# Recurrence stage: four row slots in place of three, the multipliers in the tile of the convolved rows

## The chip, the cores and the metric

The kernel is one launch on one core of one Trainium2 chip. The metric is the device time of the launch in microseconds, the median of several runs. Engines are named as the profile names them: PE (matmuls), DVE, ACT, POOL (vector, activation and general engines), SP (the queue that issues all DMAs here).

## The reference

Four sublayers, each followed by a residual add and a layer norm: a Mamba-2 mixer, a ternary linear layer with a bound on its norm, a gated linear recurrence, and a gated FFN with integer weight codes. The change is in the kernel's second stage, which computes sublayers two and three. Cut to what matters there:

```python
out = (x @ weight) * scale                       # then two factors per row from its norm
x = layernorm(x + bounded(out))                  # sublayer 2
y = gelu(x @ w_y + b_y);  xb = x @ w_x + b_x     # sublayer 3
conv = conv_b + sum(conv_w[k] * pad(xb)[:, k:k + Tn] for k in range(4))
gate_x = sigmoid(conv @ w_ig + b_ig);  gate_a = sigmoid(conv @ w_ag + b_ag)
log_a = -8 * gate_a * softplus(a_param);  a = exp(log_a)
mult = sqrt(1 - exp(2 * log_a))                  # 1 at the first row, where a = 0
h[t] = a[t] * h[t-1] + gate_x * conv * mult
x = layernorm(x + (h * y) @ w_out + b_out)
```

## The kernel before

`build` chains three stages that share the chip's memories: `mamba2`, `bounded_rg_lru` (the recurrence stage) and `gated_ffn`. Nothing is scheduled by a planner: each stage is five hand-written instruction streams, one per engine, joined by semaphores, and an engine runs its stream strictly in order. Stages overlap at their edges, because one stage's stream calls a few pieces of the following stage's.

The recurrence stage has NS = 8 steps, numbered 0 to 7; a step is 256 rows (two chunks of 128) of one of the two sequences, which alternate. Matmuls are split into high and low parts of the operands, three products for each. PE does in step s, in this order:

- `x` (L1502, `c_wx`): the projection w_x; `bounded(s+1)` (L1472, `c_wb`): the ternary layer of the next step; `y` (L1502, `c_wy`); `output(s-1)` (L1472, `c_wout`);
- `ag` (L1502, `c_wag`), which reads the convolved rows `c_cvh` and `c_cvl`; `turn(s+1)` (L1490), transposes; `ig` (L1502, `c_wig`); `turn_in(s+2)` (L1465), transposes of the raw rows of step s+2, one chunk after the other, as they were loaded into a row slot.

The elementwise chain that runs beside it: ACT makes the sigmoid `gx` (L1234) after `ig`, the exponentials `a` (L1243), the copy `c_bxh` of the transposed rows (L1211); POOL multiplies `gx` by the convolved rows `cv` (L1193, signal `s_gc`); DVE squares `a` into `mu` (`squared`, L1357); ACT takes the root in place (L1289, `s_mu`); at the top of the next step DVE (`recur`) multiplies `gx` by `mu` (L1363, `s_hchain`), scans (L1366) and multiplies by `y` (L1370); ACT and DVE split that into `c_hyh` (L1229) and `c_hyl` (L1374) for `output`; ACT rewrites `cv` for the new step (L1258), DVE adds three taps (`convolve`, L1342), ACT and DVE make `c_cvh` (L1273) and `c_cvl` (L1350) for `ag`.

In step 7 ACT makes `a` before `gx`. POOL's multiplication is then the last input that `recur(7)` waits for. Behind step 7, PE has the FFN's first three gate/up blocks `gate_up(0, 0..2)` (L1853), then `output(7)`. The gate part of block 2 waits for the FFN's first activation `d_sg` (ACT, L1753, behind the root of step 7), and its up part for the FFN's first product `d_h` (DVE, L1796, `product(0,0)`, behind `recur(7)`).

Row slots: a step's raw rows lie in a slot from their load to the step's normalised result. With three slots, the load of step s+3 is issued by SP when the result of step s (`s_ln`) is written, one step ahead of its `turn_in`. Results of steps whose slot is used again go through the tile `ob`.

Of the kernel before, what the change touches and what calls it, by code (L numbers as in the profile page):

```python
# [5 lines left out]
P = 128  # L6
D = 512
# [993 lines left out]
def bounded_rg_lru(nc, signals, psum, ident, powers, x_in, x_out, scale, vectors, b_out, W, split, last, spaces, room, ahead):  # L1001
# [5 lines left out]
    T = 256  # L1007
# [2 lines left out]
    NT = x_in.shape[0] // (B * C)  # L1010
    NS = B * NT
    M = KD
    SLOTS = 3
    TINY = 1e-7
    LIMIT = 0.99
    def sem(name):
# [37 lines left out]
    gx = sb_main("c_gx", [P, M, T], F32)  # L1054
    a = sb_main("c_a", [P, M, T], F32)
    room["mu"] = sb_main.at
    mu = sb_main("c_mu", [P, M, T], F32)
    xpre = sb_main("c_xpre", [P, M, T + 3], F32)
    xb.append(sb_main("c_xb2", [P, C, D], F32))
    bo = sb_main("c_bo", [P, D], F32)  # L1060
    room["end"] = sb_main.at
    hs = gx

    ps_t = psum[:, 0:2].rearrange("p j (k t) -> p j k t", k=KD)
    ps_o = psum[:, 2:4]
# [1 line left out]
    ps_b = psum[:, 6:8].rearrange("p q (m t) -> p q m t", m=2)  # L1067

    s_small, s_bias, s_const, s_sp, s_sp_act = (sem(n) for n in ("small", "bias", "const", "sp", "sp_act"))
    s_x = [[sem(f"x{i}_{j}") for j in range(C)] for i in range(SLOTS)]  # L1070
    s_st = [sem(f"st{j}") for j in range(C)]
    s_bt, s_bh, s_bl, s_bm, s_ob, s_ssq, s_nm, s_th, s_f = (sem(n) for n in ("bt", "bh", "bl", "bm", "ob", "ssq", "nm", "th", "f"))
    s_bvar, s_bstd, s_bln = sem("bvar"), sem("bstd"), sem("bln")
# [13 lines left out]
        return slice(j * P, (j + 1) * P)  # L1087

    def slot(s):
        return xb[s % SLOTS]  # L1090

    def finished(s):
        return ob if s + SLOTS < NS else slot(s)

    def sync(sp):
        def load_x(s):
            for j in range(C):
                wait(sp, s_ln, C * (s - SLOTS) + j + 1)
                sp.dma_start(slot(s)[:, j, :], chunk(x_in, s, j)).then_inc(s_x[s % SLOTS][j], 16)

        def store(s):
            for j in range(C):
                sp.wait_ge(s_ln, C * s + j + 1)
                sp.dma_start(chunk(x_out, s, j), finished(s)[:, j, :]).then_inc(s_st[j], 16)

        def constants():
            sp.dma_start(vec, vectors).then_inc(s_small, 16)
            sp.dma_start(scl, scale.partition_broadcast(P)).then_inc(s_small, 16)

        def main(following_stage):  # L1110
            sp.wait_ge(*last["output"])
            sp.dma_start(bo, b_out.partition_broadcast(P)).then_inc(s_bias, 16)
            load_x(2)
            for dst, src, arrived in ahead:
                sp.dma_start(dst, src).then_inc(arrived, 16)
            for s in range(NS - 2):
                if s + SLOTS < NS:
                    load_x(s + SLOTS)
                store(s)
            following_stage["small"]()  # L1120
            following_stage["load_x"](0)
            following_stage["gate_codes"]()
            store(NS - 2)
            following_stage["up_codes"]()
            following_stage["load_r"](0, 0)
            following_stage["load_r"](0, 1)
            store(NS - 1)
            following_stage["down_codes"]()
            for j in range(C):
                sp.wait_ge(s_st[j], 16 * NS)  # L1130

        return {"load_x": load_x, "constants": constants, "main": main}

    def gpsimd(pool):
        order = Order(pool, s_pool)

        def constants():
            pool.wait_ge(*last["gate"])
            pool.memset(hlast, 0.0).then_inc(s_const, 1)

        def bound(s):
            pool.wait_ge(s_ssq, C * s + C)
            order(pool.tensor_tensor(nrm, ssq, powers[:, 2:3].broadcast_to([P, C]), ALU.pow))
            pool.tensor_scalar(nm, nrm, TINY, None, ALU.max).then_inc(s_nm, 1)
            pool.wait_ge(s_nm, s + 1)
            order(pool.tensor_scalar(f, nm, TINY, None, ALU.add))
            order(pool.tensor_tensor(f, f, powers[:, 3:4].broadcast_to([P, C]), ALU.pow))
            pool.wait_ge(s_th, s + 1)
            order(pool.tensor_tensor(f, f, th, ALU.mult))
            order(pool.tensor_tensor(g, f, nrm, ALU.mult))  # L1150
            order(pool.tensor_scalar(g, g, TINY, None, ALU.max))
            order(pool.tensor_tensor(g, g, powers[:, 3:4].broadcast_to([P, C]), ALU.pow))
            order(pool.tensor_scalar(g, g, LIMIT, 1.0, ALU.mult, ALU.min))
            pool.tensor_tensor(f, f, g, ALU.mult).then_inc(s_f, 1)

        def bounded_norm(s):
            for j in range(C):
                pool.wait_ge(s_bvar, C * s + j + 1)
                inverse_root(pool, order, bmv[:, j, 1:2], powers, bmv[:, j, 2:3]).then_inc(s_bstd, 1)

        def norm(s):
            for j in range(C):
                pool.wait_ge(s_var, C * s + j + 1)
                inverse_root(pool, order, mv[:, j, 1:2], powers, mv[:, j, 2:3]).then_inc(s_std, 1)

        def out_bias(s):
            for j in range(C):
                pool.wait_ge(s_xt, C * s + j + 1)
                pool.tensor_tensor(slot(s)[:, j, :], slot(s)[:, j, :], bo, ALU.add).then_inc(s_bo, 1)

        def edges(s):
            wait(pool, s_conv, s)
            if s < B:
                pool.memset(xpre[:, :, 0:3], 0.0).then_inc(s_edge, 1)
            else:
                pool.tensor_copy(xpre[:, :, 0:3], carry[:, s % B]).then_inc(s_edge, 1)
            pool.wait_ge(s_edge, 2 * s + 1)
            pool.wait_ge(s_pre, M * s + M)
            pool.tensor_copy(carry[:, s % B], xpre[:, :, T:T + 3]).then_inc(s_edge, 1)

        def main(following_stage):
            pool.wait_ge(s_bias, 16)
            pool.wait_ge(*last["output"])
            out_bias(0)
            for s in range(NS):
                edges(s)
                if s + 1 < NS:
                    bound(s + 1)
                    bounded_norm(s + 1)
                if s:  # L1190
                    norm(s - 1)
                pool.wait_ge(s_gx, M * s + M)
                pool.tensor_tensor(gx, gx, cv, ALU.mult).then_inc(s_gc, 1)  # L1193
                if s < B:
                    wait(pool, s_hchain, s)
                    pool.memset(mu[:, :, 0:1], 1.0).then_inc(s_one, 1)
                if s + 1 < NS:
                    out_bias(s + 1)
            for m in range(EARLY):
                following_stage["low"](0, m)  # L1200
            norm(NS - 1)

        return {"constants": constants, "bound": bound, "bounded_norm": bounded_norm, "main": main}

    def scalar(act):
# [39 lines left out]
        def main(following_stage):  # L1245
            act.wait_ge(s_sp, 3)
            for s in range(NS):
                wait(act, s_conv, s)
                wait(act, s_edge, 2 * s)
                for m in range(M):  # L1250
                    act.wait_ge(s_xb, 2 * s + m // 2 + 1)
                    act.activation(xpre[:, m, 3:T + 3], ps_a[:, m // 2, m % 2, :], ACT.Identity,
                                   bias=vec[:, BX, m:m + 1]).then_inc(s_pre, 1)
                wait(act, s_gc, s)
                wait(act, s_cvl, s)
                act.wait_ge(s_pre, M * s + M)
                for m in range(M):
# [42 lines left out]
    def vector(dve):  # L1300
# [7 lines left out]
        def scaled(s):  # L1308
            if s == 0:
                dve.wait_ge(s_small, 32)  # L1310
            for j in range(C):
                dve.wait_ge(s_bm, C * s + j + 1)
                wait(dve, s_st[j], 16 * (s - SLOTS + 1))
                dve.tensor_tensor(ob[:, j, :], ps_o[:, j, :], scl, ALU.mult).then_inc(s_ob, 1)

        def bounded(s):
            dve.wait_ge(s_f, s + 1)
            for j in range(C):
                own = slot(s)[:, j, :]
                dve.wait_ge(s_x[s % SLOTS][j], 16 * (s // SLOTS + 1))  # L1320
                order(dve.scalar_tensor_tensor(out=own, in0=ob[:, j, :], scalar=f[:, j:j + 1], in1=own, op0=ALU.mult, op1=ALU.add))
                order(dve.bn_stats(bstats[:, j, :], own))
                dve.memset(hold, 0.0)
                dve.bn_aggr(bmv[:, j, 0:2], bstats[:, j, :]).then_inc(s_bvar, 1)
# [131 lines left out]
    def tensor(pe):  # L1456
        def turn_in(s):
            for j in range(C):
                pe.wait_ge(s_x[s % SLOTS][j], 16 * (s // SLOTS + 1))
                if s:  # L1460
                    pe.wait_ge(s_xl, C * (s - 1) + j + 1)
                else:
                    pe.wait_ge(*last["transposes"])
                for k in range(KD):
                    done = pe.transpose(ps_t[:, j, k, :], slot(s)[:, j, k * P:(k + 1) * P], ident)  # L1465
                done.then_inc(s_bt, 1)
# [559 lines left out]
```

## Time and profile before

| | |
|---|---|
| median of 3 runs | 1135.15 us (1133.3 to 1135.44) |
| the profiled execution, its own time | 1135.18 us |
| its span, first to last instruction | 1133.1 us |
| PE busy | 1071.9 us, 95% |
| DVE, ACT, POOL busy | 749.0 (66%), 574.2 (51%), 319.3 us (28%) |
| mean granted PE clock | 0.983 |
| the recurrence stage | about 462 to 769 us of the span |

Two microseconds of the device time lie outside the span. Shares of busy time are means over three stages; what a change in the recurrence stage is worth is read from the waits of that stage. Matmul ends are modelled, and consecutive matmuls overlap by their pipelining, so start times are what is compared.

### The profile page before, as it was taken

What the parts mean: (1) busy time and instruction counts of PE and PEld (TensorE: products, weight loads), DVE (VectorE), ACT (ScalarE), POOL (GpSimd) and SP (SyncE); (2) the same over time, 40 slices, a digit from 0 to 9 for tenths busy, and PEclk for the clock granted to TensorE, in tenths of its full rate; (3) what the DMA queues carried; (4) which work ended last, traced back from release to release, by engine and by line L of the source; (5) the groups of instructions that cost most, each with busy time, mean ns of one, the idle gap of its engine ahead of it and who ended that gap; (6) DMA issues with size and microseconds to landing.
All of it is one profiled execution on the core that took longest, in us unless ns stands there. A gap on an engine that the chain in (4) does not pass through costs nothing.

```text
span 1133.1 us, 18155 instructions
## 1 busy us (share of the span) xinstructions
PE 1071.9 (95%) x6912; PEld 934.0 (82%) x6912; DVE 749.0 (66%) x1311; ACT 574.2 (51%) x1190; POOL 319.3 (28%) x433
## 2 busy tenths in 40 slices
PE   6889999999999997889999999899999999999997
PEld 6778888888888885788998998887888888888886
DVE  6899999999999998657766687765432133223213
ACT  6856767676767673645665556563212311321220
POOL 1012223130313214343434444313312321321331
PEclk9899999999999999989999999999999999999999
DMA  5504031322313056501011101408012002002001
GB/s 197 199 3 147 31 116 47 101 60 87 108 39 127 2 201 196 194 2 29 11 38 38 38 1 38 140 19 282 15 38 75 1 19 93 1 1 75 1 1 56
DMA packets 41590, 81.22 MB, mean 72 GB/s; under 512 B 7456, under 2 KB 13472, under 8 KB 39456
## 3 DMA queue, kind: packets, MB, share of 16 engines
q1 hardware_dynamic: 41504, 80.06, 21.2%
q8 instruction: 55, 0.90, 0.3%
q14 instruction: 31, 0.25, 0.1%
HBM read 67.19 MB, written 12.85 MB: 71 GB/s over the span
## 4 chain that ended last, share of the span: by engine, by line
PE 60%; DVE 24%; ACT 7%; issue 5%; POOL 2%; DMA 1%; DVEq 0%; SPq 0%; POOLq 0%; ACTq 0%
PE banks L1853 20%; PE banks L801 12%; PE banks L1866 10%; PE banks L1502 8%; DVE a_L L658 4%; DVE a_xs L575 3%; PE banks L1472 3%; PE banks L931 2%; DVE c_gx L1366 1%; DVE c_cv L1342 1%; PE banks L923 1%; DVE a_L L672 1%; ACT c_a L1243 1%; DVE a_ygl L701 1%; PE banks L881 1%
## 5 line engine op out<-in xcount | busy, mean ns | idle before, releaser
L1753 ACT ACTIVATE d_sg<-banks,d_gs 128x512 f32<-128x512 f32 x64 | 44.0, 688 | 224.8 <-PE banks L1853 224.8
L1796 DVE SCALAR_TENSOR_TENSOR d_h<-banks,d_us,d_sg 128x512 f32<-128x512 f32 x64 | 48.1, 751 | 163.6 <-PE banks L1853 151.3
L1727 POOL TENSOR_TENSOR d_hl<-d_h,d_hh 128x512 fp32r<-128x512 f32 x64 | 83.2, 1300 | 158.3 <-ACT d_hh L1757 158.2
L575 DVE SCALAR_TENSOR_TENSOR a_xs<-a_xpre,a_cvec,a_xs 128x256 f32<-128x256 f32 x192 | 100.3, 537 | 6.4 <-ACT a_xs L446 1.8
L1866 PE MATMUL banks<-d_wd,d_hh 128*128 128x512 f32 x256 | 101.1, 395 | 0.0
L1866 PE MATMUL banks<-d_wd,d_hl 128*128 128x512 f32 x256 | 100.9, 394 | 0.0
L331 POOL TENSOR_TENSOR a_sg<-a_sg 128x512 f32<-128x512 f32 x16 | 24.5, 1533 | 221.8 <-ACT a_sg L438 221.8
L658 DVE TENSOR_TENSOR_SCAN a_L<-a_L,a_ident 128x512 f32<-128x512 f32 x64 | 78.4, 1225 | 2.2
L801 PE MATMUL banks<-a_xth,a_wxh 128*128 128x256 f32 x256 | 75.7, 296 | 0.4 <-DVE a_wxl L566 0.4
L462 ACT ACTIVATE a_xdt<-banks,a_dt 128x64 f32<-128x64 f32 x256 | 56.5, 349 | 36.4 <-PE banks L881 36.4
L801 PE MATMUL banks<-a_xth,a_wgh 128*128 128x256 f32 x256 | 74.9, 293 | 0.0
L801 PE MATMUL banks<-a_xtl,a_wxh 128*128 128x256 f32 x256 | 73.4, 287 | 0.0
L801 PE MATMUL banks<-a_xth,a_wxl 128*128 128x256 f32 x256 | 73.3, 286 | 0.0
L801 PE MATMUL banks<-a_xth,a_wgl 128*128 128x256 f32 x256 | 72.7, 284 | 0.0
L801 PE MATMUL banks<-a_xtl,a_wgh 128*128 128x256 f32 x256 | 72.7, 284 | 0.0
L801 PE MATMUL banks<-a_woh,a_ygh 128*128 128x512 f32 x128 | 54.2, 423 | 5.4 <-ACT a_gs L426 3.5
L1866 PEld LDWEIGHTS banks<-d_wd,d_hl 128*128 128x128 f32 x256 | 48.1, 188 | 11.2
L1866 PEld LDWEIGHTS banks<-d_wd,d_hh 128*128 128x128 f32 x256 | 48.2, 188 | 11.0
L801 PEld LDWEIGHTS banks<-a_xth,a_wxh 128*128 128x128 f32 x256 | 49.6, 194 | 5.1 <-issue 4.1
L801 PE MATMUL banks<-a_woh,a_ygl 128*128 128x512 f32 x128 | 52.1, 407 | 0.0
L801 PE MATMUL banks<-a_wol,a_ygh 128*128 128x512 f32 x128 | 52.0, 406 | 0.0
L1853 PE MATMUL banks<-d_xtl,d_wg_late 128*128 128x512 f32 x128 | 51.5, 402 | 0.0
(285 smaller groups left out, 3144.6 us busy)
## 6 DMA issues: line engine op xcount, KB each, us to landing
a_L<-decays SPq DMA_DIRECT2D x16, 1024.0 KB, 5.1
a_xf<-in_x SPq DMA_DIRECT2D x16, 256.0 KB, 2.9
a_xr<-in_x SPq DMA_DIRECT2D x16, 256.0 KB, 2.7
tokens<-a_xr SPq DMA_DIRECT2D x16, 256.0 KB, 4.0
c_xb<-tokens SPq DMA_DIRECT2D x16, 256.0 KB, 3.2
d_xin<-tokens SPq DMA_DIRECT2D x16, 256.0 KB, 5.0
d_r<-tokens SPq DMA_DIRECT2D x16, 256.0 KB, 2.7
d_wd_codes<-in_down_w SPq DMA_DIRECT2D x4, 1024.0 KB, 9.1
```

The costliest lines, as they stand in the source:

```text
L331: order(pool.tensor_tensor(sq[:, 0:4], sq[:, 0:4], sq[:, 4:8], ALU.add))
L462: ins = act.activation(xdt[:, j, h * HD:(h + 1) * HD], ps_t[:, q % 2, 2 * j + i // 2, i % 2 * HD:(i % 2 + 1) * HD], ACT.Copy, scale=dt[:, ...
L575: ins = dve.scalar_tensor_tensor(out=dst, in0=src[:, k:k + T], scalar=vec[:, k:k + 1], in1=dst, op0=ALU.mult, op1=ALU.add)
L658: order(dve.tensor_tensor_scan(own, own, ident4.rearrange("p h t -> p (h t)"), 0.0, ALU.mult, ALU.add))
L801: last = pe.matmul(out, lhs(i, k), rhs(c, k), start=(k, i, c) == (0, 0, 0), stop=(k, i) == (n - 1, 1))
L1472: done = pe.matmul(ps_x, x[:, k, cols(j)], wp[:, k, :], start=i == 0, stop=i == 3 * KD - 1)
L1502: done = pe.matmul(ps_x[:, q, m % 2, :], wp[:, k, m * P:(m + 1) * P], x[:, k, :], start=i == 0, stop=i == 3 * KD - 1)
L1727: pool.tensor_tensor(hl[:, m, :], h32[:, m % 2, :], hh[:, m, :].bitcast(F32), ALU.subtract).then_inc(s_hl, 1)
L1753: act.activation(sg[:, m % 2, :], ps_g[:, m % 2, :], ACT.Silu, scale=gs[:, m:m + 1]).then_inc(s_sg, 1)
L1796: dve.scalar_tensor_tensor(out=h32[:, m % 2, :], in0=ps_u[:, m % 2, :], scalar=us[:, m:m + 1], in1=sg[:, m % 2, :], op0=ALU.mult, op1=ALU. ...
L1853: ins = pe.matmul(out[:, m % 2, :], w(k, m), x[:, k, :], start=(k == 0 and x is xth), stop=(k == KD - 1 and x is xtl))
L1866: ins = pe.matmul(ps_o[:, c % 2, :], h[:, m, cols(c)], wd[:, m, :], start=(m == 0 and h is hh), stop=(m == M - 1 and h is hl))
```

## The change

A fourth row slot `c_xb3` takes the place of the tile `mu`, and `mu` becomes another name of the tile `cv`. The table `SLOT` says which slot a step uses. From this follow the waits: `squared(s)` and the memset of the first column overwrite `cv`, so they wait until POOL's multiplication has read it (`s_gc`); ACT's rewrite of `cv` in the next step waits until `recur` has read the multipliers (`s_hchain`).

```diff
-    SLOTS = 3
+    SLOT = (0, 1, 2, 3, 0, 2, 1, 0)
...
-    mu = sb_main("c_mu", [P, M, T], F32)
+    xb3 = sb_main("c_xb3", [P, C, D], F32)
     xpre = sb_main("c_xpre", [P, M, T + 3], F32)
-    xb.append(sb_main("c_xb2", [P, C, D], F32))
+    xb += [sb_main("c_xb2", [P, C, D], F32), xb3]
...
     hs = gx
+    mu = cv
...
+    def use(s):
+        return SLOT[:s + 1].count(SLOT[s])
+
+    following_use = {s: SLOT.index(SLOT[s], s + 1) for s in range(NS) if SLOT[s] in SLOT[s + 1:]}
+    earlier_use = {n: s for s, n in following_use.items()}
 
     def finished(s):
-        return ob if s + SLOTS < NS else slot(s)
+        return ob if s in following_use else slot(s)
...
             load_x(2)
+            load_x(3)
...
             for s in range(NS - 2):
-                if s + SLOTS < NS:
-                    load_x(s + SLOTS)
+                if s in following_use:
+                    load_x(following_use[s])
                 store(s)
...
             following_stage["up_codes"]()
+            store(NS - 1)
+            following_stage["down_codes"]()
+            for j in range(C):
+                sp.wait_ge(s_st[j], 16 * NS)
             following_stage["load_r"](0, 0)
             following_stage["load_r"](0, 1)
-            store(NS - 1)
-            following_stage["down_codes"]()
-            for j in range(C):
-                sp.wait_ge(s_st[j], 16 * NS)
...
                 if s < B:
-                    wait(pool, s_hchain, s)
+                    pool.wait_ge(s_gc, s + 1)
                     pool.memset(mu[:, :, 0:1], 1.0).then_inc(s_one, 1)
...
                 wait(act, s_gc, s)
+                wait(act, s_hchain, s)
                 wait(act, s_cvl, s)
...
         def squared(s):
             dve.wait_ge(s_a, M * s + M)
+            dve.wait_ge(s_gc, s + 1)
```

On SP the row loads move. In these rows `c_xb_132` is slot 0, `c_xb_138` slot 1, `c_xb_165` slot 2, `c_xb_163` the new slot 3; `tokens` is the array of rows in the chip's main memory. Before, from the load of step 2 to the store of step 5:

```order
L1099 DMA c_xb_165<-tokens 128x512 x2
...
L1099 DMA c_xb_132<-tokens 128x512 [waits c_ln] x2
L1104 DMA tokens<-c_ob 128x512 [waits c_ln] x2
L1099 DMA c_xb_138<-tokens 128x512 [waits c_ln] x2
L1104 DMA tokens<-c_ob 128x512 [waits c_ln] x2
L1099 DMA c_xb_165<-tokens 128x512 [waits c_ln] x2
L1104 DMA tokens<-c_ob 128x512 [waits c_ln] x2
L1099 DMA c_xb_132<-tokens 128x512 [waits c_ln] x2
L1104 DMA tokens<-c_ob 128x512 [waits c_ln] x2
L1099 DMA c_xb_138<-tokens 128x512 [waits c_ln] x2
L1104 DMA tokens<-c_ob 128x512 [waits c_ln] x2
```

The same place after the change, to the store of step 4:

```order
L1107 DMA c_xb_165<-tokens 128x512 x2
L1107 DMA c_xb_163<-tokens 128x512 x2
...
L1107 DMA c_xb_132<-tokens 128x512 [waits c_ln] x2
L1112 DMA tokens<-c_ob 128x512 [waits c_ln] x2
L1107 DMA c_xb_138<-tokens 128x512 [waits c_ln] x2
L1112 DMA tokens<-c_ob 128x512 [waits c_ln] x2
L1107 DMA c_xb_165<-tokens 128x512 [waits c_ln] x2
L1112 DMA tokens<-c_ob 128x512 [waits c_ln] x2
L1112 DMA tokens<-c_xb_163 128x512 [waits c_ln] x2
L1107 DMA c_xb_132<-tokens 128x512 [waits c_ln] x2
L1112 DMA tokens<-c_ob 128x512 [waits c_ln] x2
```

The loads before are those of steps 2, 3, 4, 5, 6, 7. After, step 3's goes out with step 2's; the next is step 4's (behind the result of step 0), then step 6's (behind that of step 1), step 5's (behind step 2) and step 7's (behind step 4). So steps 3, 4 and 6 are loaded earlier than before, 5 and 7 behind the same result as before.

On DVE no instruction moves; a wait is added. Here is the end of step 7 with the recurrence behind it, before:

```order
L1790 TENSOR_TENSOR d_xtl<-banks,d_xth 128x4x128 [waits d_xh] x2
L1357 TENSOR_TENSOR c_mu<-c_a 128x1024 [waits c_a]
L1363 TENSOR_TENSOR c_gx<-c_gx,c_mu 128x1024 [waits c_gc,c_mu]
L1366 SCALAR_TENSOR_TENSOR c_gx<-c_a,c_hlast,c_gx 128x256 [waits c_hchain]
L1366 SCALAR_TENSOR_TENSOR c_gx<-c_a,c_hlast,c_gx 128x256 x3
L1368 COPY c_hlast<-c_gx 128x4 [waits c_dve_order]
L1370 TENSOR_TENSOR c_gx<-c_gx,c_y 128x1024 [waits c_y,c_dve_order]
L1796 SCALAR_TENSOR_TENSOR d_h_181<-banks,d_us,d_sg 128x512 [waits d_u,d_sg]
```

The same rows after:

```order
L1801 TENSOR_TENSOR d_xtl<-banks,d_xth 128x4x128 [waits d_xh] x2
L1368 TENSOR_TENSOR c_cv<-c_a 128x1024 [waits c_gc,c_a]
L1374 TENSOR_TENSOR c_gx<-c_gx,c_cv 128x1024 [waits c_gc,c_mu]
L1377 SCALAR_TENSOR_TENSOR c_gx<-c_a,c_hlast,c_gx 128x256 [waits c_hchain]
L1377 SCALAR_TENSOR_TENSOR c_gx<-c_a,c_hlast,c_gx 128x256 x3
L1379 COPY c_hlast<-c_gx 128x4 [waits c_dve_order]
L1381 TENSOR_TENSOR c_gx<-c_gx,c_y 128x1024 [waits c_y,c_dve_order]
L1807 SCALAR_TENSOR_TENSOR d_h_181<-banks,d_us,d_sg 128x512 [waits d_u,d_sg]
```

The square now stands behind POOL's product (`c_gc`) as well as behind `a`, and writes `c_cv`.

## Rows read from the trace of the kernel before

**Rows 1.** Timeline, PE: turn_in matmuls behind a load; start, length in us, [idle before]
```profile
538.50 0.66 PE L1465 MATMUL banks<-ident,c_xb 128*128 128x128 f32 x4 [1.34 <-DMA c_xb<-tokens]
...
611.19 0.65 PE L1465 MATMUL banks<-ident,c_xb 128*128 128x128 f32 x4 [0.95 <-DMA c_xb<-tokens]
...
647.19 0.66 PE L1465 MATMUL banks<-ident,c_xb 128*128 128x128 f32 x4 [0.42 <-DMA c_xb<-tokens]
```

**Rows 2.** Timelines of ACT and PE: where ag begins in steps 2, 3, 5
```profile
558.78 1.06 ACT L1273 ACTIVATE c_cvh<-c_cv 128x1024 fp32r<-128x1024 f32 x1 [1.29 <-DVE c_cv L1342]
561.29 0.64 PE L1502 MATMUL banks<-c_cvh,c_wagh 128*128 128x256 f32 x4
567.05 1.03 PE L1490 MATMUL banks<-ident,c_xb 128*128 128x128 f32 x8
...
595.82 1.06 ACT L1273 ACTIVATE c_cvh<-c_cv 128x1024 fp32r<-128x1024 f32 x1 [1.28 <-DVE c_cv L1342]
596.93 0.74 PE L1502 MATMUL banks<-c_cvh,c_wagh 128*128 128x256 f32 x4
603.08 1.04 PE L1490 MATMUL banks<-ident,c_xb 128*128 128x128 f32 x8
...
668.39 1.06 ACT L1273 ACTIVATE c_cvh<-c_cv 128x1024 fp32r<-128x1024 f32 x1 [1.28 <-DVE c_cv L1342]
669.89 0.64 PE L1502 MATMUL banks<-c_cvh,c_wagh 128*128 128x256 f32 x4
```

**Rows 3.** Timelines of POOL and DVE: product by cv and the square, steps 3, 6
```profile
610.76 2.38 POOL L1193 TENSOR_TENSOR c_gx<-c_gx,c_cv 128x1024 f32<-128x1024 f32 x1 [3.37 <-ACT c_gx L1234]
615.43 1.29 DVE L1357 TENSOR_TENSOR c_mu<-c_a 128x1024 f32<-128x1024 f32 x1
...
720.56 2.40 POOL L1193 TENSOR_TENSOR c_gx<-c_gx,c_cv 128x1024 f32<-128x1024 f32 x1 [3.36 <-ACT c_gx L1234]
723.54 1.75 DVE L1357 TENSOR_TENSOR c_mu<-c_a 128x1024 f32<-128x1024 f32 x1 [4.56 <-ACT c_a L1243]
```

**Rows 4.** Timelines of ACT and DVE: cv rewritten, top of step 7
```profile
727.96 2.08 ACT L1258 ACTIVATE c_cv<-c_xpre,c_vec 128x256 f32<-128x256 f32 x4
728.73 1.21 DVE L1363 TENSOR_TENSOR c_gx<-c_gx,c_mu 128x1024 f32<-128x1024 f32 x1
734.15 1.06 ACT L1229 ACTIVATE c_hyh<-c_gx 128x1024 fp32r<-128x1024 f32 x1 [4.12 <-DVE c_gx L1370]
```

**Rows 5.** Timelines of DVE, POOL, ACT and PE: behind step 7
```profile
755.49 1.23 DVE L1357 TENSOR_TENSOR c_mu<-c_a 128x1024 f32<-128x1024 f32 x1 [4.50 <-ACT c_a L1243]
758.42 2.42 POOL L1193 TENSOR_TENSOR c_gx<-c_gx,c_cv 128x1024 f32<-128x1024 f32 x1 [9.21 <-ACT c_gx L1234]
759.65 1.06 ACT L1289 ACTIVATE c_mu<-c_mu 128x1024 f32<-128x1024 f32 x1
760.94 1.23 DVE L1363 TENSOR_TENSOR c_gx<-c_gx,c_mu 128x1024 f32<-128x1024 f32 x1 [4.23 <-POOL c_gx L1193]
766.26 0.74 DVE L1796 SCALAR_TENSOR_TENSOR d_h<-banks,d_us,d_sg 128x512 f32<-128x512 f32 x1
767.06 0.50 PE L1853 MATMUL banks<-d_xth,d_wu_early 128*128 128x512 f32 x1 [0.49 <-DVE d_h L1796]
```

**Rows 6.** Windows: us, busy of PE, PEld, DVE, ACT, POOL, PE clock, DMA
```profile
479.34:487.00 7.66, 5.65 (x45) 5.45 (x46) 5.75 (x4) 4.00 (x7) 6.10 (x6) 1.00 0.31 120
737.00:740.00 3.00, 3.00 (x9) 2.33 (x9) 2.93 (x8) 2.07 (x5) 0.00 (x0) 0.59 0.00 0
775.00:1120.00 345.00, 345.00 (x1507) 279.01 (x1507) 105.65 (x184) 80.34 (x134) 90.09 (x91) 1.00 0.13 45
```

**Rows 7.** Timeline, PE: first matmul of output(6), in step 7
```profile
736.52 0.79 PE L1472 MATMUL banks<-c_wouth,c_hyh 128*128 128x512 f32 x1 [4.70 <-DVE c_hyl L1374]
```

**Rows 8.** Timeline, SP: last store; the tile view, DVE: first use of d_r
```profile
776.89 1.58 SPq L1104 DMA_DIRECT2D tokens<-c_xb  x2
...
L1804 DVE TENSOR_TENSOR d_r<-d_r,d_tmp x16: 691/692/693, 834.6 to 1127.5; 128x512 f32<-128x512 f32 x16
```

More of the change, by code:

```diff
@@ L1069, in bounded_rg_lru @@
     s_small, s_bias, s_const, s_sp, s_sp_act = (sem(n) for n in ("small", "bias", "const", "sp", "sp_act"))
-    s_x = [[sem(f"x{i}_{j}") for j in range(C)] for i in range(SLOTS)]
+    s_x = [[sem(f"x{i}_{j}") for j in range(C)] for i in range(len(xb))]
     s_st = [sem(f"st{j}") for j in range(C)]
@@ L1089, in slot @@
     def slot(s):
-        return xb[s % SLOTS]
+        return xb[SLOT[s]]
+    def use(s):
+        return SLOT[:s + 1].count(SLOT[s])
+    following_use = {s: SLOT.index(SLOT[s], s + 1) for s in range(NS) if SLOT[s] in SLOT[s + 1:]}
+    earlier_use = {n: s for s, n in following_use.items()}
     def finished(s):
-        return ob if s + SLOTS < NS else slot(s)
+        return ob if s in following_use else slot(s)
     def sync(sp):
@@ L1097, in load_x @@
             for j in range(C):
-                wait(sp, s_ln, C * (s - SLOTS) + j + 1)
-                sp.dma_start(slot(s)[:, j, :], chunk(x_in, s, j)).then_inc(s_x[s % SLOTS][j], 16)
+                if s in earlier_use:
+                    sp.wait_ge(s_ln, C * earlier_use[s] + j + 1)
+                sp.dma_start(slot(s)[:, j, :], chunk(x_in, s, j)).then_inc(s_x[SLOT[s]][j], 16)
         def store(s):
@@ L1124, in main @@
             following_stage["up_codes"]()
-            following_stage["load_r"](0, 0)
-            following_stage["load_r"](0, 1)
             store(NS - 1)
@@ L1130, in main @@
                 sp.wait_ge(s_st[j], 16 * NS)
+            following_stage["load_r"](0, 0)
+            following_stage["load_r"](0, 1)
         return {"load_x": load_x, "constants": constants, "main": main}
@@ L1312, in scaled @@
                 dve.wait_ge(s_bm, C * s + j + 1)
-                wait(dve, s_st[j], 16 * (s - SLOTS + 1))
+                wait(dve, s_st[j], 16 * (s - 2))
                 dve.tensor_tensor(ob[:, j, :], ps_o[:, j, :], scl, ALU.mult).then_inc(s_ob, 1)
@@ L1319, in bounded @@
                 own = slot(s)[:, j, :]
-                dve.wait_ge(s_x[s % SLOTS][j], 16 * (s // SLOTS + 1))
+                dve.wait_ge(s_x[SLOT[s]][j], 16 * use(s))
                 order(dve.scalar_tensor_tensor(out=own, in0=ob[:, j, :], scalar=f[:, j:j + 1], in1=own, op0=ALU.mult, op1=ALU.add))
@@ L1458, in turn_in @@
             for j in range(C):
-                pe.wait_ge(s_x[s % SLOTS][j], 16 * (s // SLOTS + 1))
+                pe.wait_ge(s_x[SLOT[s]][j], 16 * use(s))
                 if s:
```

## The prediction

> **What bounds the kernel now.** I began with the granted clock and PE's busy share, then asked for the stretch behind the recurrence: from 775 to 1120 us PE is busy 345.00 of 345.00 us at clock 1.00 [rows 6]. So whatever moves the start of that stretch moves the end of the kernel by as much, and the question is only what PE loses before it.
>
> The waits for row loads came next. In the timeline of PE the second chunk of `turn_in` sits behind the load in four places: 1.34 us for step 3's rows, 0.95 for step 5's, 0.42 for step 6's [rows 1], and one like these for step 7's. Step 4's rows come in time. That is what a fourth slot can attack.
>
> Last, what would stop PE if a load did not. `ag` needs `c_cvh` from the chain through DVE and ACT. In step 2 `c_cvh` is ready at 558.78 + 1.06 = 559.84, and `ag` starts at 561.29, because PE itself is late, by the wait of 1.34. In step 3 it is ready at 596.88 and `ag` starts at 596.93: here the chain sets the pace, with the load of step 4's rows in time [rows 2]. There is a second cost in that state. `c_cvl` comes one DVE instruction after `c_cvh`, so `ag`, which runs 567.05 - 561.29 = 5.76 us when both are ready, takes 603.08 - 596.93 = 6.15 us [rows 2]. PE and the chain are level within a few tenths, so neither alone is the bound.
>
> **The change part by part.**
>
> *Loads of steps 3, 4 and 6 earlier.* Step 3's wait of 1.34 us goes. `ag` of step 2 could start at 561.29 - 1.34 = 559.95; the chain allows 559.84 [rows 1, 2]. The chain does not gain from the early load: it starts from `ig`, and the raw rows enter it only with `c_bxh`, which ACT copies behind the exponentials anyway. So `ag` gains 1.34, and is now as close behind `c_cvh` as in step 3, which costs it most of 6.15 - 5.76 = 0.39; I take 0.34. Net 1.0 us. Step 4's early load removes no wait. For step 6, 0.42 us goes: `ag` of step 5 starts at 669.89 with `c_cvh` ready at 669.45, so it can move 0.42, and then pays the same stall of nearly 0.39 [rows 1, 2]. Net 0.05. The waits for steps 5 and 7 stay: their loads go out behind the same results, and these move with PE. Sum: **-1.0 us**. Bounds: -1.76 if every removed microsecond counts (1.34 + 0.42), -0.6 if a second stall of 0.39 shows up.
>
> The Trainium skill has a rule for this, in "DMA: Bandwidth & Descriptors", Rules for kernel authors: issue a DMA early and wait late, so that its fixed cost overlaps. Its "Perfetto Trace Analysis", Optimization Strategy, adds that the same gap repeated on the saturated engine can mean too few buffers. Both read these gaps as a buffer shortage; by them the gain would be the whole 1.76 us, where the rows on `c_cvh` leave 1.0.
>
> *The square behind POOL's product, steps 0 to 6.* In steps 0 to 5 DVE first makes the low part of step s+2's rows. In step 3 POOL ends at 610.76 + 2.38 = 613.14 and the square starts at 615.43, a margin of 2.3 us. In step 6 there is no such work; POOL ends at 722.96, the square starts at 723.54, a margin of 0.58 [rows 3]. Cost nothing; without that cover step 6 would pay what POOL is late, in the chain to `output(6)`. In steps 0 and 1 DVE already waits for the memset behind the same product.
>
> *The rewrite of `cv` behind `s_hchain`.* In ordinary steps DVE's product by `mu` runs while ACT makes four `xpre`, so nothing is late. At the top of steps 6 and 7 DVE converts FFN weights first. For step 7 the product ends at 728.73 + 1.21 = 729.94, so ACT starts `cv` then and not at 727.96 and ends near 732.0. ACT's next work, `c_hyh`, starts at 734.15 after 4.12 us of idleness [rows 4]. Hidden; `convolve` comes later still.
>
> *The square behind POOL's product, step 7.* Here `gx` is made last, so the order inverts. Before: square at 755.49, root at 759.65, both finished (760.71) when POOL's product ends at 758.42 + 2.42 = 760.84; DVE's product starts at 760.94 [rows 5]. After: the square starts behind 760.84, takes 1.23; the root takes 1.06; with the handovers of a few hundredths each the product starts at about 763.3. That is 2.35 us later. `recur(7)` has no slack: `d_h` at 766.26 follows it, and PE waits for it already, 0.49 us, at 767.06 [rows 5]. So the up part of block 2 starts near 769.4. The activations behind the root are late by about as much, which delays the gate part of the same block less than that; it adds nothing to the sum. `c_hyl` is ready before that up part ends, as now. Sum: **+2.35 us**. Bounds: +2.29 (1.23 + 1.06, no handover) to +2.8, if half a microsecond is lost at the following products.
>
> *SP.* One load more stands ahead of the FFN's early codes, which DVE converts only in steps 5 and 6. The FFN's first residual rows `d_r` move behind the last store. That store is issued at 776.89, and the first use of `d_r` is at 834.6 [rows 8]: even several microseconds for the down codes and the landing leave some 45. Late up codes wait for `s_hy` of step 7, 2.35 - 1.0 us later, and PE, which wants them later by the same amount, never waits in that stretch [rows 6]. Cost nothing.
>
> **Sum:** 1135.18 (the profiled execution's own time: span 1133.1 and 2.1 around it) - 1.0 + 2.35 = **1136.5 us**. The median of the runs shown, 1135.15, is the same within 0.03, so this is also the forecast of the median: 0.12% slower, within the 0.2% (2.3 us) that a measurement of this kernel can tell from no change.
>
> **The rivals.**
>
> *The clock falls in the new gap (slower).* The place is block 2 of the FFN behind step 7: PE's 0.49 us of idleness grows to about 2.8, in two pieces around the gate part. After 4.70 us of idleness ahead of `output(6)` [rows 7] the granted clock from 737 to 740 is 0.59, which means mostly the lower level, 1.2 GHz [rows 6]; with the half microsecond ahead of it that costs about 3.0 x 0.41 + 0.25 = 1.5 us. Against it: with 7.66 - 5.65 = 2.0 us idle in one stretch the clock stayed at 1.00 [rows 6]. The new gap lies between. If it falls: 1136.5 + 1.5 = 1138.0 us, 0.25% slower. It decides as soon as the fall costs over 0.9 us. The Trainium skill, "TensorE: Matmul & The Clock Gate", HAM oscillation, warns of this: gaps put the array back to half rate and each return is paid again. It speaks against the change; the row on `output(6)` agrees. Chance 0.2.
>
> *All the removed waits count.* If `ag` does not pay for `c_cvl`, or the chain moves with PE, the gain is 1.76: 1135.8 us. For it: the wait of 1.34 disappears in full. Against it: `ag` in step 3. Chance 0.13.
>
> *The end of step 7 is hidden (faster or level).* If PE's work behind step 7 absorbs the late root, the sum is 1134.2 us, and with all waits counted 1133.4. For it: two and a half gate/up blocks stand between `ig` and the first instruction that needs it. Against it: PE waits for `d_h` already now. Chance 0.1.
>
> *The added waits show in other steps.* A late POOL product in step 6, or DVE and POOL in each other's way, since a square of 1.29 us takes 1.75 there [rows 3]. Half a microsecond in two or more steps: 1137.5 to 1138.5 us. Chance 0.1.
>
> *The change doesn't do what it says:* the rows of steps 3 and 6 still arrive late. They are issued a step or more earlier, so this would need a stuck queue; then 1137.5. Chance 0.02.
>
> **How the numbers follow.** The forecast has 0.45. Runs before spread over 2.1 us, and half-rate stretches of PE fall differently in each run, so each case carries about 1 us to either side. The range 1134.2 to 1138.7 reaches from the hidden end to the fallen clock with a little over. Slower by over 0.2% (above 1137.4): most of the clock's 0.2, half of the added waits and a sixth of the forecast, 0.29. Faster by over 0.2% (below 1132.9): a part of the hidden end, 0.06. The rest, 0.65, is within.
>
> **What would show it.** In the profile after: no idle PE at `turn_in` for steps 3 and 6, some 1 us for 5 and 7; `ag` of steps 2 and 5 starting within 0.1 us of `c_cvh` and taking about 6.1 us; the start of `ig` in step 3 one microsecond earlier. In step 7, the square starting as POOL's product ends, and PE idle over 2 us ahead of the up part of block 2. The prediction is wrong if that gap is not there, if PE's clock drops behind it, or if the square waits for POOL in steps 1 to 6.

## The result, and the profile after

In the comparison of the two kernels, twelve runs of each, the changed one took 1137.87 us (median; 1136.12 to 1139.52) and the one before 1134.31 us (1132.73 to 1135.44). The ratio is 1.0026, 95% interval 1.0017 to 1.0036: slower by about 0.26%. (The medians alone lie 3.56 us apart, 0.31%. Each ratio in this text comes with its interval from the record and is not the quotient of the medians beside it.) The profiled execution took 1136.12 us, with a span of 1134.4 us.

First the loads. Timeline of PE after the change, all waits for row loads that are left from `turn_in(3)` to the end of step 6 (start, length in us; idle time before in brackets), and the first matmuls of `turn_in(6)`:

```profile
610.05 0.66 PE L1476 MATMUL banks<-ident,c_xb 128*128 128x128 f32 x4 [1.01 <-DMA c_xb<-tokens]
...
645.03 1.04 PE L1476 MATMUL banks<-ident,c_xb 128*128 128x128 f32 x8
...
682.62 0.66 PE L1476 MATMUL banks<-ident,c_xb 128*128 128x128 f32 x4 [0.96 <-DMA c_xb<-tokens]
```

Steps 3 and 6 no longer wait, steps 5 and 7 still do [rows 1]. Timelines of ACT and PE, where `ag` begins in step 2 and in step 5:

```profile
558.58 1.06 ACT L1283 ACTIVATE c_cvh<-c_cv 128x1024 fp32r<-128x1024 f32 x1 [1.29 <-DVE c_cv L1352]
559.70 0.74 PE L1513 MATMUL banks<-c_cvh,c_wagh 128*128 128x256 f32 x4
...
667.23 1.06 ACT L1283 ACTIVATE c_cvh<-c_cv 128x1024 fp32r<-128x1024 f32 x1 [1.28 <-DVE c_cv L1352]
668.35 0.75 PE L1513 MATMUL banks<-c_cvh,c_wagh 128*128 128x256 f32 x4
```

In step 2 `c_cvh` is ready at 559.64 and `ag` starts 0.06 us later, where 1.45 us lay between before [rows 2]; the stage's next section (`turn`) starts at 565.85, so `ag` takes 6.15 us and not 5.76.

Now the end of step 7. Timelines of POOL, DVE, ACT and PE:

```profile
757.24 2.42 POOL L1202 TENSOR_TENSOR c_gx<-c_gx,c_cv 128x1024 f32<-128x1024 f32 x1 [9.19 <-ACT c_gx L1243]
...
759.76 1.23 DVE L1368 TENSOR_TENSOR c_cv<-c_a 128x1024 f32<-128x1024 f32 x1 [9.94 <-POOL c_gx L1202]
762.12 1.22 DVE L1374 TENSOR_TENSOR c_gx<-c_gx,c_cv 128x1024 f32<-128x1024 f32 x1 [1.13 <-ACT c_cv L1299]
767.43 0.74 DVE L1807 SCALAR_TENSOR_TENSOR d_h<-banks,d_us,d_sg 128x512 f32<-128x512 f32 x1
...
761.02 1.06 ACT L1299 ACTIVATE c_cv<-c_cv 128x1024 f32<-128x1024 f32 x1 [2.57 <-DVE c_cv L1368]
...
764.23 0.47 PE L1864 MATMUL banks<-d_xth,d_wg_early 128*128 128x512 f32 x1 [0.70 <-ACT d_sg L1764]
768.23 0.50 PE L1864 MATMUL banks<-d_xth,d_wu_early 128*128 128x512 f32 x1 [1.90 <-DVE d_h L1807]
```

The square stands behind POOL's product and the root behind the square. From the end of POOL's product (759.66) to DVE's product by the multipliers it is 2.46 us, where it was 0.10 [rows 5]. PE idles 0.70 us ahead of the gate part of block 2 and 1.90 us ahead of its up part, where it was 0.49 in all. By start times, which don't hang on modelled ends, `output(7)` follows `gate_up(0,0)` by 14.29 us (770.19 - 755.90) and not by 11.96 (769.03 - 757.07).

Windows behind the gap (busy PE, PEld, DVE, ACT, POOL; granted clock; DMA). In this execution the clock stays up:

```profile
768.00:773.00 5.00, 4.77 (x21) 3.88 (x22) 2.82 (x4) 2.97 (x5) 3.47 (x3) 1.00 0.85 274
773.00:777.00 4.00, 4.00 (x19) 3.22 (x18) 2.54 (x6) 0.00 (x0) 1.68 (x3) 1.00 0.49 185
```

The median of the changed kernel lies 1.75 us above this execution. Two parts of the program are therefore measured apart in every profile below, and both are free of what happens ahead of the stage. **A** runs from the first matmul of `turn_in(3)` to the first matmul of `gate_up(0,0)` (the end of `ig` in step 7), **B** from there to the end of the span. (Spans are printed to a tenth, so differences of up to 0.1 us in B are rounding.) Here A went from 220.51 to 219.74 and B from 376.03 to 378.50.

| kernel | span | A | B | `output(7)` takes | clock fell behind the gap |
|---|---|---|---|---|---|
| before | 1133.1 | 220.51 | 376.03 | 5.56 | no |
| changed | 1134.4 | 219.74 | 378.50 | 5.60 | no |
| changed, again (`after_again`) | 1138.2 | 219.53 | 380.10 | 6.71 | yes |
| changed, third | 1135.9 | 219.85 | 380.01 | 6.53 | yes |
| changed, fourth | 1137.5 | 219.82 | 380.08 | 6.06 | yes |
| `mu_only` | 1134.4 | 220.41 | 378.54 | 5.60 | no |
| `early5` | 1136.7 | 219.20 | 380.00 | 6.62 | yes |
| `filled`, three profiles | 1135.9, 1135.1, 1132.4 | 219.79, 219.96, 219.89 | 378.39, 378.49, 378.43 | 5.56, 5.60, 5.60 | no |
| `last_mu` | 1130.9 | 219.78 | 376.03 | 5.55 | no |
| `last_mu_convert` | 1126.5 | 217.47 | 376.12 | 5.56 | no |
| `all_three` | 1131.2 | 217.00 | 376.12 | 5.56 | no |
| `before_convert` | 1128.6 | 218.09 | 376.11 | 5.55 | no |

What is left of each span, its start to `turn_in(3)`, is 532.9 to 538.6 us in these 14 executions, although the code there is all but the same. It is why a single time says little here, and A and B much. Steps 0 and 1, where the memset of the first column has a new wait too, lie in that part. From the first matmul of `x(0)` to `turn_in(3)` the twelve profiles with the shared tile took 72.0 to 75.1 us and the two without it 74.3 and 74.6, at mean clocks of 0.93 to 0.98: no cost of the change is seen there, and one of some tenths could not be.

### The profile page after: what moved, and what is told of

Its sections match the earlier page's. It is cut to its first block, busy times and chain, and to the rows that moved or that the text cites. A ratio compares the mean times of both kernels' runs of the same rounds, so it can differ in the third digit from the quotient of the medians.

```text
span 1134.4 us, 18168 instructions
## 1 busy us (share of the span) xinstructions
PE 1078.2 (95%) x6912; PEld 939.1 (83%) x6912; DVE 749.5 (66%) x1311; ACT 573.3 (51%) x1190; POOL 320.5 (28%) x433
## 4 chain that ended last, share of the span: by engine, by line
PE 59%; DVE 25%; ACT 6%; issue 6%; POOL 2%; DMA 1%; DVEq 0%; SPq 0%; POOLq 0%; ACTq 0%
PE banks L1864 20%; PE banks L1877 10%; PE banks L1513 10%; PE banks L801 9%; DVE a_L L658 5%; PE banks L1483 5%; DVE a_xs L575 4%; PE banks L931 2%; DVE a_ygl L701 1%; DVE a_L L672 1%; DVE c_gx L1377 1%; PE banks L923 1%; DVE c_cv L1352 1%; ACT c_a L1252 1%; DVE a_ex L646 1%
## 5 line engine op out<-in xcount | busy, mean ns | idle before, releaser
L1864 PE MATMUL banks<-d_xth,d_wu_early 128*128 128x512 f32 x128 | 50.7, 396 | 1.9 <-DVE d_h L1807 1.9
```

The costliest lines, as they stand in the source:

```text
L1864: ins = pe.matmul(out[:, m % 2, :], w(k, m), x[:, k, :], start=(k == 0 and x is xth), stop=(k == KD - 1 and x is xtl))
```

## The experiments

The theory was that of the prediction: the early loads are worth under a microsecond, the serial end of step 7 costs 2.35, and the rest is the clock or noise. The rivals: all waits count; the added waits cost in other steps too; the clock falls in the new gap.

**The changed kernel again** (`after_again`; no edit).

> The changed kernel once more, for a second profile and more times. In its first profile the recurrence gains 0.8 us and the end of step 7 loses 2.35 us, which is +1.2 to +1.5 us on the time before, but the medians of twelve runs lie 3.5 us apart. Theory A (the clock falls behind the new gap in part of the executions): +2 to +4 us in the median, and the profile shows either a clock of 1.00 in the first blocks of the FFN and a time near the low end, or one near half for some microseconds and a time about 1.5 us higher. Theory B (the two medians lie apart because of the stage before, whose half-rate stretches differ by run): the median comes back to +1 to +2 us, with no difference behind step 7 between the profiles.

It took 1136.7 us against 1134.77, ratio 1.0012 (0.9998 to 1.0026). Its profile has the same gaps, 0.70 and 1.90 us, but behind them:

```profile
770.00:775.00 5.00, 4.57 (x14) 3.64 (x15) 3.01 (x4) 3.16 (x5) 3.26 (x3) 0.69 0.83 262
775.00:779.00 4.00, 4.00 (x18) 3.27 (x17) 1.56 (x4) 0.00 (x0) 1.39 (x3) 0.96 0.52 201
```

A clock of 0.69 means that much of the window ran at 1.2 GHz: 14 matmuls in place of 21. `output(7)` takes 6.71 us, B is 1.6 us longer than in the first profile. The rival's fall does happen, in some executions. The difference of the medians, 1.93 us, lies just below what the first theory asked for and within what the second did; the profile decides, since behind step 7 the two executions differ.

**Only the shared tile** (`mu_only`): three slots in the order of before, `mu` in `cv`. Like all edits but that of `before_convert`, this one is made to the changed kernel.

```diff
-    SLOT = (0, 1, 2, 3, 0, 2, 1, 0)
+    SLOT = (0, 1, 2, 0, 1, 2, 0, 1)
...
-            load_x(3)
```

> The multipliers share the tile of the convolved rows, but rows are loaded into three slots in the order of the kernel before. By the prediction's sum: +2.35 us on the kernel before, and up to 1.5 us more if the clock falls behind the gap; PE's waits for loads as before (1.3, 0.0, 0.9, 0.4, 1.0 us). If the loss belonged to the loads, this kernel would be within 0.5 us of the kernel before.

1136.5 us, ratio 1.0023 (1.0009 to 1.0037). A is 220.41, within 0.1 of before: the waits that the shared tile adds in steps 2 to 6 cost nothing. PE waits 1.16, 0.21, 1.02, 0.48 and 1.12 us for the rows of steps 3 to 7, near the 1.3, 0.0, 0.9, 0.4 and 1.0 expected. B is 378.54, the whole 2.5 us. So A's gain in the changed kernel belongs to the slots, and B's loss to the shared tile.

**Step 7's multipliers in another tile** (`last_mu`): in step 7 alone they lie in slot 3, which is free by then, and the square does not wait.

```diff
-    mu = cv
+    multipliers = [cv] * (NS - 1) + [xb3.rearrange("p c (m t) -> p (c m) t", m=M // C)]
...
-            dve.wait_ge(s_gc, s + 1)
+            if multipliers[s] is cv:
+                dve.wait_ge(s_gc, s + 1)
```

> As the changed kernel, but step 7 squares into the fourth slot, which is free by then, and does not wait for POOL's product; steps 0 to 6 keep their multipliers in the tile of the convolved rows. By the prediction's sum the 2.35 us behind step 7 are gone and the gain of the early loads stays: 0.6 to 1.2 us faster than the kernel before, 2.3 us or, with a clock that falls behind the gap, up to 4 us faster than the changed one. PE waits about 0.5 us for the first FFN product, as before. The rival, that the loss comes from the early load of step 3 at the head of the stage or from the waits in steps 0 to 6, expects no or little gain on the changed kernel.

1132.88 us, ratio 0.9980 (0.9969 to 0.9991): faster than before. Timelines of DVE, ACT, POOL and PE at the end of its step 7:

```profile
753.29 1.23 DVE L1369 TENSOR_TENSOR c_xb<-c_a 128x1024 f32<-128x1024 f32 x1 [4.50 <-ACT c_a L1252]
758.74 1.23 DVE L1375 TENSOR_TENSOR c_gx<-c_gx,c_xb 128x1024 f32<-128x1024 f32 x1 [4.22 <-POOL c_gx L1202]
...
757.45 1.06 ACT L1299 ACTIVATE c_xb<-c_xb 128x1024 f32<-128x1024 f32 x1
...
756.21 2.42 POOL L1202 TENSOR_TENSOR c_gx<-c_gx,c_cv 128x1024 f32<-128x1024 f32 x1 [9.21 <-ACT c_gx L1243]
...
764.86 0.50 PE L1865 MATMUL banks<-d_xth,d_wu_early 128*128 128x512 f32 x1 [0.49 <-DVE d_h L1808]
```

Square and root are done before POOL's product ends, as in the kernel before [rows 5], PE waits 0.49 us, and B is 376.03, as before, while A keeps the gain of the slots. One wait in one step is the whole loss. By A and B alone it should win 0.73 us over before. The timed 1.9 us is more than that and than the 0.6 to 1.2 expected, and the interval ends at 1.0; what the rest is stays open.

**Step 5's rows a step earlier** (`early5`): the slot order (0, 1, 2, 3, 0, 1, 2, 0), all else as changed.

> As the changed kernel with the slots in the order 0, 1, 2, 3, 0, 1, 2, 0, so that step 5's rows are loaded one step earlier as well; step 7's stay late. This takes away the wait of 1.0 us in step 3. If the chain through DVE and ACT sets the pace where PE does not wait (the prediction), ag of step 4 moves by 0.95 us, pays 0.3 to 0.4 of it for the low part, and the kernel gains 0.5 to 0.7 us on the changed one. If every removed wait counts in full, it gains 1.0 us.

1136.86 us, ratio 1.0013 (1.0002 to 1.0024). Of the four waits at `turn_in` only step 7's is left, 1.15 us. A is 219.20, between 0.33 and 0.65 us better than in the four profiles of the changed kernel; expected were 0.5 to 0.7. The time is no lower than that of the changed kernel. The clock fell again.

**Dummy matmuls in the gap** (`filled`): two ahead of the gate part of block 2, seven ahead of its up part; work that is added, and nothing reads what it writes.

```diff
+                    if i == 0 and m == 2:
+                        for _ in range(2 if out is ps_g else 7):
+                            pe.matmul(psum[:, 0], w(0, m), xth[:, 0, :], start=True, stop=True)
                     pe.wait_ge(used, M * i + m - 1)
```

> The changed kernel with nine matmuls more, whose results nothing reads: two ahead of the gate part and seven ahead of the up part of the FFN's block 2, inside the gaps of 0.7 and 1.9 us that PE has there. Same waits, about 1.9 us less idleness. In two of four profiles with the gap left open the clock fell behind it and cost 1.5 us. If the idleness is what makes it fall, this profile shows the clock at 1.00 from the first FFN block to the end of output(7), and the median is 0.4 to 1.0 us below that of the changed kernel. If the fall has another cause, half of such profiles fall still, and the median is the same or 0.1 us higher.

1136.33 us against 1134.21, ratio 1.0016 (1.0002 to 1.003). Expected was a median 0.4 to 1.0 us below that of the changed kernel. That did not come out: the medians lie 2.12 us above before with the gap filled and 1.93 or 3.56 with it open, and these differ by less than the intervals are wide, so the timed runs don't decide. Its profile:

```profile
763.00:768.00 5.00, 4.86 (x22) 3.59 (x21) 4.16 (x7) 3.25 (x4) 0.00 (x0) 1.00 0.00 0
768.00:773.00 5.00, 4.67 (x21) 3.47 (x20) 3.91 (x5) 2.79 (x4) 1.93 (x2) 1.00 0.54 142
773.00:777.00 4.00, 4.00 (x19) 3.27 (x18) 2.09 (x5) 0.63 (x1) 2.89 (x4) 1.00 0.89 342
```

PE is busy through the gap, the up part waits 0.33 us, and the clock is 1.00.

**How often it falls.** Two more profiles each of the changed kernel and of the filled one, one execution each:

> The changed kernel once more, one profile. The question is how often the granted clock falls behind the gap of some 2.6 us ahead of the up part of block 2. If the fall is a matter of chance from execution to execution, as two profiles of four so far say, either outcome can come: 1.00 in the windows behind the gap and about 366.1 us from the up part to the end of the span, or a window below 0.95 and about 367.7 us.

> The changed kernel with nine dummy matmuls in the gap, one profile. If idleness of PE is what lets the clock fall, the clock is 1.00 in every window of block 2 and output(7), and output(7) takes 5.6 us, as in its first profile. If the fall comes whatever PE does there, it is seen in about half of the profiles, and output(7) takes 6.2 to 6.7 us.

> As the third profile of the changed kernel: a fall costs about 1.5 us behind the up part of block 2, no fall costs nothing; with a chance near one half, one of the two further profiles should show it.

> As the second profile of the kernel with dummy matmuls: clock 1.00 and 5.6 us for output(7) if idleness is the cause; three profiles without a fall beside about half of the open ones with one would be weak evidence for it, one fall would refute it.

Windows of PE alone (busy, clock, DMA share, GB/s) behind the gap, of the changed kernel's third profile:

```profile
766.00:768.00 2.00, 0.33 (x2) 1.00 0.00 0
768.00:771.00 3.00, 2.77 (x9) 0.75 0.76 186
771.00:774.00 3.00, 3.00 (x10) 0.68 0.99 369
774.00:777.00 3.00, 3.00 (x15) 1.00 0.37 150
```

and of its fourth:

```profile
769.50:772.50 3.00, 2.75 (x8) 0.66 0.67 182
772.50:775.50 3.00, 3.00 (x12) 0.77 1.00 377
```

With the two further ones of the filled kernel at 1.00 throughout, the count is: gap open (changed kernel four times, `mu_only`, `early5`), four falls in six; gap filled, none in three; gap as before (before, `last_mu` and three below), none in five. The cost of a fall is B's step from 378.5 to between 380.0 and 380.1, 1.5 to 1.6 us, each time. Three filled profiles against six open ones are few: had the fall come with its rate of four in six whatever PE does, three without one would have a chance of 1 in 27; if only the four falls in these nine profiles are taken as given, the chance that all four land among the six open ones is 15 in 126, one in eight. With the five profiles of a short gap counted as well, four in six beside none in eight, it is 15 in 1001. So that the fall goes with the wider gap is well borne out, and that PE's idleness is what matters in that gap is likely, not shown.

**The conversions ahead of the square.** In steps 5 and 6 DVE converts FFN weights between the square and the product. Here it does so before `turn_in` and the square, where it idles 4.56 us for `a` [rows 3], together with `last_mu` (`last_mu_convert`), with that and the slots of `early5` (`all_three`), and alone in the kernel before (`before_convert`).

```diff
+                if NS - 4 < s < NS - 1:
+                    for i in range(4 * (s - NS + 3), 4 * (s - NS + 4)):
+                        following_stage["convert"](i)
                 if s + 2 < NS:
                     turn_in(s + 2)
...
                 squared(s)
-                if NS - 4 < s < NS - 1:
-                    for i in range(4 * (s - NS + 3), 4 * (s - NS + 4)):
-                        following_stage["convert"](i)
```

> As last_mu (four slots, step 7's multipliers in the fourth slot), and the FFN weights that DVE converts in steps 5 and 6 are converted ahead of turn_in and of the square, where DVE is idle for about 5 us, and not between the square and the recurrence. If PE's idleness of 4.7 us ahead of output(6) is the recurrence of step 6 held up by these four conversions (3.5 us), it shrinks to about 1.2 us and the half-rate matmuls behind it become fewer: 3.5 to 5.5 us faster than last_mu. If the chain is held by the root or by POOL's product, 0.5 us at most.

> last_mu_convert with the slot order of early5, so that only step 7's rows are loaded late. early5 gained 0.4 to 0.5 us on the changed kernel between ig of step 1 and the end of step 7 in the profiles; the same is expected here on last_mu_convert, below what the times can tell. By the prediction's view of step 5 (the chain was behind PE because of its four conversions), the wait of 1.0 us for step 7's rows now reaches ag of step 6: PE and not c_cvh should be what ag starts behind there.

> The kernel before (three slots, multipliers of their own) with the conversions moved as in last_mu_convert. It gains what they cost: 3.5 to 5.5 us on the kernel before. The difference to last_mu_convert is then what the fourth slot is worth: 0.7 to 1.0 us by the sum of the prediction's first part.

Against 1134.21 us of before: 1129.69 (0.9977; 0.9961 to 0.9994), 1131.27 (0.9976; 0.9961 to 0.9991) and 1132.67 (0.9986; 0.997 to 1.0003). The first two beat the kernel before; among themselves and `last_mu` nothing can be told apart, and the third can't be told from before. By A the moved conversions are worth 2.3 us in the kernel with four slots (219.78 to 217.47) and 2.4 in the kernel before (220.51 to 218.09), not the 3.5 to 5.5 expected of both. The difference between those two, 0.62 us for the fourth slot, is a little less than the 0.7 to 1.0 expected; the slots of `early5` give 0.47 more, as expected, and `ag` of step 6 then takes 5.76 us, as where both its inputs are ready. Timelines of DVE, POOL, ACT and PE in step 6 of `last_mu_convert` show where the rest went:

```profile
715.15 0.68 DVE L1796 TENSOR_SCALAR d_wg_early<-d_wg_early_codes 128x1024 fp32r<-128x1024 int32 x1
715.75 2.89 DVE L1796 TENSOR_SCALAR d_wu_early<-d_wu_early_codes 128x1024 fp32r<-128x1024 int32 x1
718.62 2.26 DVE L1369 TENSOR_TENSOR c_cv<-c_a 128x1024 f32<-128x1024 f32 x1
722.00 1.25 DVE L1375 TENSOR_TENSOR c_gx<-c_gx,c_cv 128x1024 f32<-128x1024 f32 x1 [1.13 <-ACT c_cv L1299]
...
715.64 2.46 POOL L1202 TENSOR_TENSOR c_gx<-c_gx,c_cv 128x1024 f32<-128x1024 f32 x1 [3.38 <-ACT c_gx L1243]
718.06 3.98 POOL L1178 TENSOR_TENSOR c_xb<-c_xb,c_bo 128x512 f32<-128x512 f32 x2
...
716.87 1.71 ACT L1252 ACTIVATE c_a<-c_a,c_spt 128x256 f32<-128x256 f32 x4
720.91 1.06 ACT L1299 ACTIVATE c_cv<-c_cv 128x1024 f32<-128x1024 f32 x1 [1.02 <-DVE c_cv L1369]
...
729.83 0.50 PE L1484 MATMUL banks<-c_wouth,c_hyh 128*128 128x512 f32 x1 [2.92 <-DVE c_hyl L1386]
```

The fourth conversion starts 0.11 us behind POOL's product, and takes 2.89 us where the one ahead of it takes 0.68. That costs nothing here: it ends with ACT's `a` (716.87 + 1.71 = 718.58), which the square at 718.62 waits for in any case, 0.03 us behind it as in the kernel before. What is lost is behind the square. It takes 2.26 us and not the 1.75 of before [rows 3], beside POOL's next work, and then the root is bare: DVE waits 1.13 us for it, where in the kernel before it ran while DVE converted. From the square's start to the product by the multipliers it is 3.38 us (722.00 - 718.62) and was 5.19 (728.73 - 723.54) [rows 3, 4]. These 1.81 us are what the idle time ahead of `output(6)` shrinks by, from 4.70 [rows 7] to 2.92. The other half microsecond of A comes earlier: `ag` of step 6 takes 5.75 us and not 6.15, and starts 0.15 us sooner behind `turn_in(3)`.

## Why the prediction was right, and where not

**The loads (-1.0): right in mechanism, a little large.** A fell by 0.77 us, and lies at 219.5 to 220.0 in all eight profiles with these slots, mean 219.80, which is 0.7. Two terms were sized a few tenths off. `ag` of step 2 gained 1.19 us relative to `turn_in(3)` (24.73 to 23.54) and not 1.34, because `c_cvh` came 0.2 us later on the same scale; and it paid the full 0.39 for `c_cvl`, not 0.34. Step 6's 0.42 gave 0.40 and cost 0.39: nothing, not 0.05. That PE and the chain are level was right, and the rival that all removed waits count (1.76 us) is refuted. The Trainium skill's rule that was weighed there ("DMA: Bandwidth & Descriptors", Rules for kernel authors), to issue a DMA early and wait for it late so that its fixed cost overlaps, agrees with the trace: the waits of 1.34 and 0.42 us are gone. It does not say that the time comes back in full, as the prediction read it, and here it did not.

**The square in steps 0 to 6 (nothing): right.** In step 6 POOL ends at 719.39 + 2.41 = 721.80 and the square starts at 722.37, released by ACT's `a`: a margin of 0.57, as before. `mu_only` gives A within 0.1 us of before, which refutes the rival of waits in other steps for steps 2 to 6.

**The rewrite of `cv` (hidden): right.** Rows of ACT at the top of step 7, after the change:

```profile
728.86 2.08 ACT L1268 ACTIVATE c_cv<-c_xpre,c_vec 128x256 f32<-128x256 f32 x4 [2.18 <-DVE c_gx L1374]
732.99 1.06 ACT L1238 ACTIVATE c_hyh<-c_gx 128x1024 fp32r<-128x1024 f32 x1 [2.05 <-DVE c_gx L1381]
```

ACT waits 2.18 us for DVE's product and still idles 2.05 before `c_hyh` [rows 4].

**The end of step 7 (+2.35): right.** `output(7)` comes 14.29 - 11.96 = 2.33 us later behind `gate_up(0,0)`; `last_mu` takes that away. The delay of the gate part, 0.70 us, is contained in it, as said. Of B's 2.47 us that leaves 0.14: `output(7)` takes 5.60 us and not 5.56, and the rest is within the rounding of two spans.

**SP (nothing): right.** The last store is issued at 778.09, `d_r` is first used at 835.9, and from 775.79 to 1120 us PE is busy 344.21 of 344.21 us at clock 1.00.

**The clock: the step that failed.** The prediction set it at nothing in the forecast and gave it 0.2, on the row in which 2.0 us of idleness left the clock at 1.00 [rows 6]. Its place and its price were right: it falls in block 2, and costs 1.5 to 1.6 us where 1.5 was worked out. Its frequency was not: four of six profiles. It is no case beside the forecast, but a part of the mean, and by the prediction's own signs ("if PE's clock drops behind it") four of six executions speak against it.

The row that carried the 0.2 was one execution. The same idle time ahead of `ag` of step 0, 1.96 to 1.97 us, stands in all 14 profiles; over the 5 us from the start of that `ag` the clock is 0.66 or 0.67 in eight of them and 1.00 in six, the kernel before among the six. The trace of before itself had a warning some 25 us ahead of that row, where PE idled in three short pieces. Its timeline and windows of PE there and behind the row, then a window of the changed kernel:

```profile
451.80 0.66 PE L1490 MATMUL banks<-ident,c_xb 128*128 128x128 f32 x4 [0.84 <-DVE c_xb L1330]
453.73 0.66 PE L1490 MATMUL banks<-ident,c_xb 128*128 128x128 f32 x4 [1.27 <-DVE c_xb L1330]
454.85 0.38 PE L860 MATMUL banks<-a_ones,a_sg 128*128 128x1 f32 x2 [0.46 <-POOL a_sg L333]
...
451.00:456.10 5.10, 2.57 (x15) 1.00 0.00 0
456.10:459.50 3.40, 3.40 (x10) 0.50 0.00 0
481.30:486.30 5.00, 4.95 (x39) 1.00 0.08 27
...
483.06:488.06 5.00, 4.95 (x27) 0.67 0.43 170
```

Behind pieces of 0.84, 1.27 and 0.46 us, none as long as the new 1.90, the clock is 0.50 from 456.10 to 459.50. Two rows that point either way would have asked for a chance near one half.

The right sum, by the profiles: -0.7 (A) + 2.4 (B) - 0.33 (time outside the span, below) + 4/6 x 1.5 (clock) = +2.4 us, 1.0021. The two timings of the changed kernel, 1.0026 and 1.0012, have their intervals around that; the medians of the first lie a further 1.2 us apart, which no run here explains.

So the number holds partly by luck. The forecast of 1136.5 us was 1.4 below the median and inside the range, but it started from 1135.18, and in the comparison the kernel before took 1134.31: as a difference it was +1.35, and +3.56 was measured, then +1.93. The upper part of the range was there for the fallen clock and the added waits, not for the forecast itself. Of its signs "slower by over 0.2%", to which it gave 0.29, came out in the first timing, and the second leaves it open.

## What to carry to other kernels

Before two tiles share their memory, look for the step in which the order of reader and writer is inverted: here seven steps took the sharing for nothing and the eighth, the last, paid more than the extra buffer brought; a third place for that one step (a buffer that is free by then) kept the gain. A removed load wait is worth what the next input of the waiting engine leaves, so find when that input is ready before counting the wait. And when a change opens a gap on PE behind which the clock might fall, count the fall by its share of executions, from several profiles: one profile shows either of two times. A gap of like size elsewhere that left the clock alone in one execution says as little: the one used here was followed by a fall in eight of 14.

## What the runs showed of the hardware

The same gap (0.70 us idle, 2.1 us of matmuls, 1.90 us idle) was followed by half-rate matmuls in four executions and not in two; the three profiles in which PE ran dummy matmuls there showed none. The single gap of 1.96 to 1.97 us in step 0 was followed by them in eight of 14. There the fall cost nothing: the next section of PE, which waits for other engines, starts 9.46 or 9.47 us behind `ag` in all 14. What decides it from one execution to the next, no run here shows.

A DVE instruction beside a POOL one can take over four times as long: the conversion of 128x1024 elements took 0.68 us alone and 2.89 us (2.90 in `before_convert`) when it began 0.05 to 0.11 us behind POOL's product of 2.4 us, ending some half microsecond behind it. The Trainium skill, "SBUF — State Buffer", Who interferes with whom, says that DVE and GpSimd (POOL here) share one pair of ports under an exclusive lock, so that beside a DVE instruction that takes both pairs the one that comes second is blocked and not slowed. The trace agrees with blocked: the 2.89 us end 0.54 us behind POOL's end at 718.10; the third conversion, which began ahead of POOL's product, still took 0.68. The square of step 6 stands beside POOL's next work too: 1.75 us before the change [rows 3], 1.76 after it and 2.20 to 2.26 where the conversions were moved, against 1.23 in step 7, where POOL is idle.

The device time outside the span was 1.68 to 1.80 us in all timed runs of the kernels whose step 7 has the serial square (the changed one, `mu_only`, `early5`, `filled`), and 1.98 to 2.18 us in those of the kernel before, `last_mu` and the three with moved conversions. That third of a microsecond hides a part of the loss, and nothing here explains it.
